# Attention: the place of the weighing and of the projection item among the four score tiles of a half unit

## The reference

```python
def _L1_attn_ref(x, Wq, Wk, Wv, Wo, bo):      # x: (8, 1024, 384), 12 heads of 32
    q = (x @ Wq.T).reshape(b, n, H, HD).transpose(0, 2, 1, 3)
    k = (x @ Wk.T).reshape(b, n, H, HD).transpose(0, 2, 1, 3)
    v = (x @ Wv.T).reshape(b, n, H, HD).transpose(0, 2, 1, 3)
    scores = jnp.einsum('bhqd,bhkd->bhqk', q, k) * SCALE
    probs = jax.nn.softmax(scores, axis=-1)
    out = jnp.einsum('bhqk,bhkd->bhqd', probs, v)
    out = out.transpose(0, 2, 1, 3).reshape(b, n, c)
    return out @ Wo.T + bo
...
t = t + _L1_attn_ref(_ln_t(t), ...)           # _ln_t: layer norm over the channels of a token
```

## Time and profile before

| | |
|---|---|
| median of 3 runs | 2680.7 us |
| the profiled execution | 2679.47 us |
| its span in the profile | 2677.7 us |
| TensorE (PE) busy | 2514.2 us, 94% of the span, 35488 matmuls |
| VectorE (DVE) busy | 1867.8 us, 70% |
| ScalarE (ACT) busy | 1540.2 us, 58% |
| GpSimd (POOL) busy | 1499.0 us, 56% |
| granted TensorE clock, mean | 0.985 |

### The profile page before, as it was taken

One profiled execution on the slowest core, in us unless ns is written; L12 is line 12 of the kernel. 1 busy time (PEld: TensorE's weight loads), 2 busy tenths in 40 slices (PEclk: granted clock), 3 DMA queues, 4 the chain that ended last, 5 costly groups with the idle time before them and its releaser, 6 DMA issues. The chain is left out here.

```text
span 2677.7 us, 82792 instructions
## 1 busy us (share of the span) xinstructions
PE 2514.2 (94%) x35488; PEld 1306.5 (49%) x35488; DVE 1867.8 (70%) x2390; ACT 1540.2 (58%) x2649; POOL 1499.0 (56%) x1155
## 2 busy tenths in 40 slices
PE   3899889999999999999999999988899999999999
PEld 3555445555555545545555545544344444444444
DVE  5898688898998898888988988986333333333332
ACT  2444256676676676676676766777444444444443
POOL 3567467887887787788788788878101011010110
PEclk9899999999999999999999999999999999999999
DMA  3223142113112121131131131120110010010100
GB/s 121 74 106 146 59 114 58 34 34 105 34 57 81 34 97 46 36 111 35 39 103 36 37 108 42 34 100 3 69 42 30 24 47 23 24 46 23 47 23 24
DMA packets 68511, 154.53 MB, mean 58 GB/s; under 512 B 13521, under 2 KB 17550, under 8 KB 68174
## 3 DMA queue, kind: packets, MB, share of 16 engines
q1 hardware_dynamic: 68174, 149.63, 17.6%
HBM read 60.74 MB, written 37.75 MB: 37 GB/s over the span
## 5 line engine op out<-in xcount | busy, mean ns | idle before, releaser
L1349 DVE TENSOR_REDUCE b_mxp<-b_mx 128x4 f32<-128x2048 f32 x384 | 877.2, 2284 | 117.9 <-PE b_mx L1197 115.3
L1483 ACT ACTIVATE s_stage<-b_st 128x512 f32<-128x512 f32 x864 | 490.2, 598 | 293.1 <-PE b_st L1181 278.1
L1593 POOL TENSOR_TENSOR b_pair<-s_stage 128x512 f32<-128x512 f32 x384 | 505.6, 1337 | 196.2 <-ACT s_stage L1483 195.6
L1181 PE MATMUL b_st<-b_qst,b_kst 97*32 97x256 f16 (+2 forms) x10944 | 558.5, 277 | 27.4 <-DMA b_qst<-b_shift 9.8
L1838 DVE TENSOR_TENSOR c_gs<-c_g,c_gs 128x512 f16<-128x512 f32 x192 | 132.8, 692 | 486.6 <-ACT c_gs L1918 486.6
L1483 ACT ACTIVATE b_ex<-b_st 128x512 f32<-128x512 f32 x672 | 388.5, 597 | 89.1 <-PE b_st L1181 67.8
L1763 PE MATMUL c_hid<-s_z,c_wi 128*128 128x512 f16 x1728 | 406.7, 381 | 6.0 <-DVE c_wi L1876 6.0
L1181 PEld LDWEIGHTS b_st<-b_qst,b_kst 97*32 97x32 f16 (+2 forms) x10944 | 246.7, 95 | 337.0 <-ACT s_stage L1483 120.7
L1778 PE MATMUL c_acc<-c_gs,c_wo 128*128 128x512 f16 x1728 | 404.0, 379 | 0.0
L1593 POOL TENSOR_TENSOR b_pair<-b_ex 128x512 f32<-128x512 f32 x288 | 360.1, 1279 | 0.1
L1914 ACT ACTIVATE c_g<-c_hid,c_bias 128x512 f32<-128x512 f32 x192 | 131.4, 684 | 364.4 <-PE c_hid L1763 364.1
(11 more groups left out here) (187 smaller groups left out, 3220.5 us busy)
## 6 DMA issues: line engine op xcount, KB each, us to landing
s_first_x<-after_conv SPq DMA_DIRECT2D x9, 1536.0 KB, 7.2
b_qst<-b_staged0q SPq DMA_DIRECT2D x192, 64.0 KB, 2.4
b_kst<-b_staged0k SPq DMA_DIRECT2D x192, 64.0 KB, 2.0
b_v<-b_vstaged SPq DMA_DIRECT2D x24, 512.0 KB, 3.5
after_attention<-s_first_x SPq DMA_DIRECT2D x8, 1536.0 KB, 6.0
c_x<-after_attention SPq DMA_DIRECT2D x16, 768.0 KB, 5.5
out<-c_ob SPq DMA_DIRECT2D x16, 768.0 KB, 6.8
s_next_x<-after_conv SPq DMA_DIRECT2D x7, 1536.0 KB, 10.0
```

Of the source, the lines that this page charges most:

```text
L1181: last = nc.tensor.matmul(st[n % NST][c:c + tile, j * QUERIES:(j + 1) * QUERIES], kst[g][0:depth, s, kt * P + c:kt * P + c + tile], qst[g] ...
L1349: nc.vector.reduce_max(mxp[x % 2][:, w // 2, :, w % 2], mx[:, :, :], AX_X).then_inc(mx_taken, 1)
L1483: nc.scalar.activation(ex[u % 2][e][s][:, :], st[n % NST][:, :], ACT.Exp, scale=SCALE).then_inc(exp_ready, 1)
L1593: nc.gpsimd.tensor_tensor(pair[u % 2][s][:, :], ex[u % 2][0][s][:, :], ex[u % 2][1][s][:, :], ALU.add).then_inc(pair_ready, 1)
```

## The change

In `unit` of the TensorE block only, for each half: behind score tiles 0 and 1 (and the mean product) come now the values and the sums, in every half; then the variance product, score tiles 2 and 3 one after the other; then the half's whole share of the item (pieces 0 to 5, 5 to 9, or 0 to 9) in one piece, with the item's waits ahead of it; then the wave. The other engines' orders are not touched.

```diff
-                    pieces = (0, 0), (0, 0)
+                    share = None
                     if begin and whole is None:
-                        pieces = ((0, 3), (3, 5)) if e == 0 else ((5, 8), (8, 9))
+                        share = (0, 5) if e == 0 else (5, 9)
                     elif begin and e == whole:
-                        pieces = (0, 5), (5, 9)
+                        share = 0, 9
                     weighed = lagging(b, u, 2 - e) and (*before(b, u, 2 - e), 1 - e)
-                    if pieces[0][1]:
-                        if pieces[0][0] == 0:
+                    if weighed:
+                        weigh_values(*weighed)
+                        weigh_sums(*weighed)
+                    if load and u in VAR_AT and e == 1:
+                        var(b + 2, VAR_AT.index(u))
+                    scores(b, u, e, 2, tile)
+                    scores(b, u, e, 3, tile)
+                    if share:
+                        if share[0] == 0:
                             if u == FIRST:
                                 pe.wait_ge(exp_ready, FILLS * (IU * b + u) + 1)
                             begin()
-                        part(*pieces[0])
-                    elif weighed:
-                        weigh_values(*weighed)
-                    if load and u in VAR_AT and e == 1:
-                        var(b + 2, VAR_AT.index(u))
-                    scores(b, u, e, 2, tile)
-                    if pieces[0][1]:
-                        part(*pieces[1])
-                    elif weighed:
-                        weigh_sums(*weighed)
-                    scores(b, u, e, 3, tile)
-                    if weighed and pieces[0][1]:
-                        weigh_values(*weighed)
-                        weigh_sums(*weighed)
+                        part(*share)
                     if has_wave(b, 2 * u + e):
                         wave(b, 2 * u + e)
```

## The result

The kernel after the change takes 2751.05 us (median of 4 runs, 2747.05 to 2752.57); the kernel before, run beside it on the same chip, 2679.64 (4 runs, 2678.08 to 2682.94). The ratio is 1.026, interval 1.0248 to 1.0274: 71 us slower, where the forecast was 57 slower. The profiled execution took 2752.57 us with a span of 2750.8, so 73.1 over the one before in both.

What follows compares the result with a forecast made beforehand. TensorE sets the pace, VectorE close behind. Per image -3.4 - 0.5 + 8.8 + 1.6 + 1.6 - 0.4 = +7.7; seven images +54, ends +4: +58 on 2679.5, so 2737 us, range 2703 to 2763.

Steps and rivals of the forecast that it cites:

- the likeliest case: Whole kernel: the copy ahead of exponential 7 stalls TensorE; 2737 us, with 2715 to 2757 from the bounds, chance 0.65.
- Halves with an item, 3.70 and 3.48: Five-piece halves take 3.70 instead of 3.79 us, four-piece 3.48 instead of 3.63: 0.24 per unit, -3.4 us per image.
- The stall of 0.80 in eleven halves, +8.8: Copy holds exponential 7, so the next unit's score tile 1 waits 0.80 us for its bank: +8.8 us per image.
- full-array halves: Units 22 and 23, halves with V's matmuls: 3.84 instead of 3.95 us despite one more tiling switch, -0.5 per image.
- rival B: Nearly the same: stalls fall where TensorE waits for VectorE anyway; +3 us per image, 2703 us, chance 0.1.
- Unit 2, forecast -0.24: Unit 2, counted among 14 units with an item whose two halves together gain 0.24 us.
- Units 6 and 7, forecast nothing: Their gains or losses count nothing, as unit 8 waits for shift rows and starts as long after unit 5 as before.
- unit 8, -0.24 with its stall absorbed: Unit 8 gains 0.24 us as a unit with an item; the stall after unit 7 is absorbed by the shift-row wait.
- +1.6 for halves without an item: Units 3, 13, 16, 17: tile 2 starts at 1.75 instead of 1.31 us, delaying the next half; +1.6 us per image.
- the move in unit 15: Values wait earlier for the move out of pv: +0.85 us in unit 15, within about +1.6 for moves per image.
- Rival C: Worse: VectorE becomes the bound as stage_low waits for the copy; +0.5 in some eight units, +28, 2765 us, chance 0.18.
- The signs that were named: Trace: copy about 3.4 into second halves, tile 1 at about 1.0, ScalarE waits 60 to 80 us, shorter out-projection units.

Runs made afterwards that it cites:

- run 1: Kernel after the change, with ScalarE's copy of a spread item moved from behind exponential 6 to behind exponential 7: 2718.99 us.
- run 4: Kernel after the change, with GpSimd's residual addition cut to 16 of 512 columns, so its output lacks most of that addition: 2711.05 us.
- run 5: Kernel after the change, with GpSimd's residual addition whole but moved behind the first pair addition of the next unit: 2767.28 us.
- run 7: Kernel before the change, with SP's order in unit 6 as shift rows, load of the image after next, then residual store and load: 2669.32 us.
- run 6: Kernel after the change, with SP's store and load of the residual moved behind the shift rows of unit 6: 2755.19 us.
- run 3: New TensorE order in second halves only, the old order in first halves: 2725.17 us, 1.0161 of the kernel before.
- Run 10: Kernel after the change, with copy behind exponential 7, SP's order of shift rows, load, residual, and residual additions behind the next unit's first pair addition: 2688.15 us.
- run 8: Kernel before the change, with ScalarE's copy of a spread item moved behind exponential 7: 2691.66 us.
- run 11: Kernel before the change, with SP's order of shift rows, load, residual, and the new order only in first halves of units spreading an item: 2662.81 us.
- run 12: New order in both halves of spread-item units only, with copy behind exponential 7, SP's order of rows, load, residual, and late residual additions: 2674.57 us.

## Why the prediction was right, and where it was off

The sign and the range held: 2751 lies within 2703 to 2763, and the likeliest case, the copy in front of exponential 7, is what happened. That it came within 14 us is in part luck: stalls and moves were put too high, and the collision and the clock, which cost more than that, were not in the sum at all. By its steps:

- **Halves with an item, 3.70 and 3.48:** exact, to 0.01 us, wherever nothing waits (units 1, 4, 5, 12), and 3.85 for the 3.84 of the full-array halves (second halves of 22 and 23). The steps read from the earlier trace rows can be put together in another order.
- **The stall of 0.80 in eleven halves, +8.8:** its mechanism is shown by run 1. It is 0.70, as the copy starts 3.28 into the half (1034.47 to 1037.75) instead of 3.37. It stands in nine halves (units 0, 9, 10, 13, 16, 20 to 23) and to 0.3 in 15 and 19: 9 x 0.70 + 2 x 0.3 = 6.9. Where the wave already waited for VectorE (first halves of 19 and 20: 4.52 and 4.35 before), the stall took that wait's place and the unit got no longer. This is rival B's mechanism, in two units only.
- **Unit 2, forecast -0.24:** +1.41. This is the step that failed. The text says that VectorE and ScalarE "keep their orders", and takes their durations from the trace of before. The order was kept, but the beginnings moved by some tenths against GpSimd's, and one product went from 0.42 to 1.47 us, which the maximum and the wave had no slack for. The Trainium skill (GPSIMD Engine Reference, Specifications) states that GpSimd's SBUF interface is shared with VectorE, with contention for VectorE's instructions with two SBUF inputs; the product has two, and run 4 agrees (0.42 us in units 2 and 6 instead of 1.44 to 1.48, the second half 3.48 instead of 5.59). The page has no price; the row's is 1.05 us.
- **Units 6 and 7, forecast nothing; unit 8, -0.24 with its stall absorbed:** +0.97, +0.12 and +0.67, so 2.0 more. The argument held that what unit 6 loses, unit 8's wait takes up, as the rows are late anyhow. But the rows became later too: from the end of unit 5 to the start of unit 8 it is 18.29 us instead of 17.20. It is GpSimd's residual additions that set this: with them short the wait is 0.8 to 1.2 us (run 4), with them later 4.6 to 5.0 (run 5). And the clock was at its lower level behind this wait in three images and behind that of unit 6 in one. In run 7 the wait is gone, and in runs 4 and 7 no inner image has the lower clock; in run 6 both only moved to unit 9.
- **Unit 3:** +1.24. Of the +1.6 for halves without an item in 3, 13, 16 and 17 its share came as worked out: score tile 1 of its second half starts 3.41 after the start of its first (2.92 + 0.49) where 3.42 was forecast, 0.27 later than before. Its second half, with a whole item, is longer by another 0.38 when second halves alone are new (4.94 for 4.56, run 3), for which the forecast had nothing. The other 0.6 is the clock behind the wait in unit 2, in images 6 and 7.
- **Moves and halves without an item in 13, 16, 17:** +1.26, +1.11, +0.92, with 0.70 in 13 and 16 being the stall, so 1.9 in all. For the move in unit 15 the forecast had +0.85, and the unit is 0.02 shorter. Run 10 shows that with the three causes mended these units, 3 and 5 keep the new order behind the old.
- **Rival C** had the right engine for a part, and the wrong place: VectorE didn't become late by `stage_low` in every unit, but by a product that ran longer beside GpSimd's addition in two units.
- **The signs that were named:** the copy at 3.28, tile 1 at 0.93 and the halves of 3.48 came as said; the waits for ScalarE are 44.6 us, where 60 to 80 were said. Two of the signs spoke against the forecast: the waits for the maximum grew beyond 25 us (40.7), the mark set for C, and of the out-projection units, which should be shorter, units 2 and 3 are longer.

Per image: forecast +7.7, less 1.9 for the stalls, +1.65 for unit 2, +2.0 for 6 to 8, +0.85 for unit 3 (1.24 less the 0.4 that is its share of the +1.6), and -0.5 in the rest (14, 15, 18, 11 and others) make 9.8. The clock's 1.7 is within these terms. Six inner images give 2.1 x 6 = 12.6 of the 15.6 us by which the profiled executions differ from the forecast (73.1 and 57.5); the ends, 14.3 instead of 11.7, give nearly all the rest. What stays open is what makes the clock fall. Behind the waits for the shift rows in the kernel after it fell at 2.14, 2.46 and 2.61 us and not at 2.08; but it also fell behind two of the eleven waits of 1.80 in units 2 and 6 of the inner images and behind the one of 3.04. In run 8 it fell behind 1.92 and 2.00, and in run 1 a wait of 2.83 was followed by none. So the length of the wait alone doesn't decide. No run was made that changes it by itself.

## What to carry to other kernels

Before work is moved on one engine, list for every other engine's in-order queue what stands behind an instruction that the move makes wait: here a copy of 0.6 us, for which ScalarE had to wait 0.4, held an exponential that held a bank, and cost 32 us. List too what runs beside what: a start that moves by 0.2 us can fall behind another engine's instruction. Price each half of a reordering alone. Here the first halves with an item gain, the second lose more than that in the units behind them. The DMA queue's order mended by itself gives 11 us (run 7), and only the part of the new order that gains goes below that (run 11). A removed wait is often just handed to the next due thing: runs 5 and 6 each removed the wait they aimed at, and gained nothing.

## What of the hardware was not expected

- **Durations depend on a start by a tenth of a microsecond.** A product on VectorE with two SBUF inputs takes 0.42 us when it begins 0.13 ahead of a GpSimd addition (which then takes 1.44 us instead of 1.28), and 1.47 when it begins 0.09 behind one. It is not slowed by a share: in the kernel after, 15 of these products began 0.08 to 0.66 behind an addition, took between 0.90 and 1.48 us, and each of them ended 0.28 us after the addition did. The small shift steps behave alike. One that takes 0.17 alone took 1.20 in the trace after and 1.34 in the trace before, and ended 0.03 after GpSimd's residual addition.
- **One wait can cost twice.** A wait of 2.46 us within a kernel that is otherwise busy was followed by 3.4 us at a granted clock of 0.52, with 44 matmuls where 80 fit, and so 1.57 us more in that half (5.26 against 3.69). A wait of 1.88 at the same place left the clock at 1.00; one of 1.92 in run 8 was followed by 0.59 over 3.6 us, and one of 1.80 in unit 2 by 0.50 over 3.3 us. The inner images of runs 4, 7, 10, 11 and 12, which have no such wait for the maximum in units 2 and 6 and none or a short one for the rows, have no stretch at the lower clock.
